# Moving the causal mask of an attention stage from a TensorE product into VectorE's row-minimum instructions

## The reference

```
def attn(x, latent_w, latent_b, Wd_w, Wd_b, out_w, out_b):   # x is layer-normalised
    Wdkv = x @ latent_w + latent_b                            # [b, t, 72], keys and values at once
    q = einsum('btc,hcl->bhtl', x, Wd_w) + Wd_b               # 16 heads
    scores = einsum('bhtl,bsl->bhts', q, Wdkv) / 4            # sqrt(256 / 16)
    scores = where(tril(t, t), scores, -inf)                  # causal
    y = einsum('bhts,bsl->bhtl', softmax(scores), Wdkv)
    return concat_heads(y) @ out_w + out_b
x = x + attn(layernorm(x)); x = x + birwkv(layernorm(x), ctx, ctx, w, u); x = x + experts(layernorm(x))
```

## Time and profile before

| | |
|---|---|
| Runs | 595.64, 602.27, 596.83 us; median 596.83 |
| Span of the profiled execution | 602.4 us (no other time of it is given) |
| PE busy | 524.7 us, 87% |
| DVE busy | 363.1 us, 60% |
| ACT busy | 329.2 us, 55% |
| POOL busy | 314.9 us, 52% |
| 24 to 345 us, the attention: PE, DVE, ACT, POOL busy | 297.19, 221.41, 198.31, 178.85 of 321 us |

### The profile page before, as it was taken

One profiled execution on the slowest core, in us unless ns is written; L12 is line 12 of the kernel. 1 busy time (PEld: TensorE's weight loads), 2 busy tenths in 40 slices (PEclk: granted clock), 3 DMA queues, 4 the chain that ended last, 5 costly groups with the idle time before them and its releaser, 6 DMA issues.

```text
span 602.4 us, 10421 instructions
## 1 busy us (share of the span) xinstructions
PE 524.7 (87%) x3490; PEld 455.9 (76%) x3490; DVE 363.1 (60%) x749; ACT 329.2 (55%) x944; POOL 314.9 (52%) x277
## 2 busy tenths in 40 slices
PE   0898978998999999999899595688997999999691
PEld 0786756876878878888678264588997999999691
DVE  3376696684888776746547634478884787650010
ACT  4376765773677755765554324254784777651120
POOL 3444877535473587622635644064637476644442
PEclk9999999998999999999988879589999999999797
DMA  6405354454365444534302447333958889989610
GB/s 189 166 3 123 58 65 101 57 72 87 57 96 102 65 59 66 105 77 70 64 26 91 111 140 226 124 96 83 280 154 287 210 238 228 235 253 358 176 27 0
DMA packets 53087, 75.65 MB, mean 126 GB/s; under 512 B 10185, under 2 KB 41674, under 8 KB 52778
## 3 DMA queue, kind: packets, MB, share of 16 engines
q1 hardware_dynamic: 43106, 63.91, 41.8%
q0 software_dynamic: 9040, 10.93, 9.6%
q10 hardware_dynamic: 888, 0.15, 0.1%
HBM read 49.29 MB, written 9.49 MB: 98 GB/s over the span
## 4 chain that ended last, share of the span: by engine, by line
PE 39%; DMA 22%; issue 12%; DVE 9%; POOL 9%; ACT 4%; SPq 3%; POOLq 1%; another core or an unknown queue 0%; ACTq 0%
DMA out<-Y,TK 14%; PE P L672 10%; PE PO L796 8%; PE P L750 6%; PE P L768 5%; DMA qT<-qP 3%; POOL out L1717 3%; PE P L758 3%; DMA zP<-ZT 2%; SPq L577 2%; POOL cxa L1690 2%; ACT EB L1011 2%; POOL xs L1676 1%; DMA arena<-wd 1%; PE P L743 1%
## 5 line engine op out<-in xcount | busy, mean ns | idle before, releaser
L1011 ACT ACTIVATE EB<-P,small 128x128 f32<-128x128 f32 x256 | 90.7, 369 | 79.3 <-DVE small L1235 60.1
L1633 POOL TENSOR_TENSOR EB<-EB,small 128x512 f32<-128x512 f32 x64 | 78.9, 1241 | 98.4 <-DVE small L1239 98.2
L672 PE MATMUL P<-GT,WF 128*128 128x256 f32 x768 | 100.8, 290 | 7.2 <-DVE GT L1162 2.6
L672 PEld LDWEIGHTS P<-GT,WF 128*128 128x128 f32 x768 | 96.4, 196 | 8.2 <-DVE GT L1162 3.1
L1717 POOL DMA_INDIRECT out<-Y,TK x39 | 67.4, 1729 | 66.3 <-DMA out<-Y,TK 28.9
L768 PE MATMUL P<-PT,V 128*72 128x512 f32 x128 | 68.7, 619 | 11.2 <-ACT PT L1016 10.1
L750 PEld LDWEIGHTS P<-KT,qT 72*128 72x128 f32 x512 | 67.7, 194 | 12.6 <-DMA qT<-qP 6.8
L750 PE MATMUL P<-KT,qT 72*128 72x128 f32 x512 | 68.9, 278 | 5.4 <-DMA qT<-qP 4.7
L796 PE MATMUL PO<-Ow,zP 128*128 128x256 f32 x270 | 71.2, 407 | 2.0 <-DMA zP<-ZT 1.9
L1250 DVE COPY ZT<-P 72x512 f32<-72x512 f32 x64 | 43.3, 677 | 45.1 <-PE P L768 42.1
L796 PEld LDWEIGHTS PO<-Ow,zP 128*128 128x128 f32 x270 | 52.9, 205 | 17.2 <-issue 10.7
(11 more groups left out here) (237 smaller groups left out, 950.6 us busy)
## 6 DMA issues: line engine op xcount, KB each, us to landing
WR<-wf SPq DMA_DIRECT2D x27, 512.0 KB
arena<-wf SPq DMA_DIRECT2D x24, 512.0 KB
qT<-qP SPq DMA_DIRECT2D x63, 128.0 KB
WS<-wf SPq DMA_DIRECT2D x12, 512.0 KB, 7.4
zP<-ZT SPq DMA_DIRECT2D x80, 72.0 KB
zP<-ZT SPq DMA_DIRECT2D x80, 36.0 KB
X<-x SPq DMA_DIRECT2D x4, 512.0 KB, 6.9
cxa<-ctxin SPq DMA_DIRECT2D x4, 512.0 KB, 5.8
```

Source lines behind the costliest of these rows:

```text
L672: r = e.matmul(o, lt(a), rt_(b), start=start and n == 0, stop=stop and n == 2, skip_group_check=skip)
L1011: e.activation(EB[i][:, j, :], S[:, 128 * j:128 * j + 128], ACT.Exp, bias=NM[i][:, j:j + 1], accum_out=SM[i][:, j:j + 1]).then_inc(s_exp, 1)
L1633: e.tensor_tensor(EB[i][:, :, :], EB[i][:, :, :], SM[i].unsqueeze(2).broadcast_to([128, 4, 128]), ALU.mult).then_inc(s_prob, 1)
```

## The change

The scores are now negated: the query weights and biases are scaled by -0.25 where they were scaled by 0.25. A tile `later` (128 x 128 fp32, 0 on and below the diagonal and 2 to the 100th above it) takes the place of `maskr` and `identr`. PE no longer writes a mask into the bank. DVE adds `later` to each head's negated scores in an instruction that also writes the sum into `EB` (SBUF) and the row minimum into `NM`: four instructions for a unit where one stood. ACT's exponentials read and write `EB` in place, with scale -1 and the minimum as bias, and each waits for its own head's minimum. Since DVE writes `EB`, the wait for the transposes of unit n-3 is DVE's now; and since DVE is the last reader of the bank, PE waits for DVE (`s_max`) where it waited for ACT.

```diff
-        maskr = sb("maskr", [128, 4, 128], f32r, s1)
-        identr = sb("identr", [128, 128], f32r, s1)
+        later = sb("later", [128, 128], fp32, s1)
...
             def scores(n):
...
-                pe.wait_ge(s_cact, ACTC["mask"])
-                pe.wait_ge(s_exp, 4 * (n - 1))
-                e.matmul(S[:, :], identr[:, :], maskr[:, :, :].rearrange("p a b -> p (a b)"), start=True, stop=False, skip_group_check=True)
+                pe.wait_ge(s_max, 4 * (n - 1))
...
                 for j in range(4):
                     p = e.matmul(S[:, 128 * j:128 * j + 128], qT[k % 2][:, 4 * hq + j, c:c + 128], KT[g % 2][:, r:r + 128],
-                                 start=False, stop=True, skip_group_check=True)
+                                 start=True, stop=True)
...
-            ac.wait_ge(s_cpool, POOLC["ident"])
-            e.activation(identr[:, :], ident[:, :], ACT.Copy).then_inc(s_cact, 1)
-            ac.wait_ge(s_cpool, POOLC["mask"])
-            e.activation(maskr[:, :, :], mf, ACT.Copy).then_inc(s_cact, 1)
...
             def exps(n):
-                S, i = SB[n % 2], n % 3
-                ac.wait_ge(s_max, n + 1)
-                ac.wait_ge(s_T, n - 2)
+                i = n % 3
                 for j in range(4):
-                    e.activation(EB[i][:, j, :], S[:, 128 * j:128 * j + 128], ACT.Exp, bias=NM[i][:, j:j + 1], accum_out=SM[i][:, j:j + 1]).then_inc(s_exp, 1)
+                    ac.wait_ge(s_max, 4 * n + j + 1)
+                    e.activation(EB[i][:, j, :], EB[i][:, j, :], ACT.Exp, scale=-1.0, bias=NM[i][:, j:j + 1], accum_out=SM[i][:, j:j + 1]).then_inc(s_exp, 1)
...
             def row_max(n):
+                i = n % 3
+                ve_.wait_ge(s_cpool, POOLC["mask"])
+                ve_.wait_ge(s_T, n - 2)
                 ve_.wait_ge(s_S, n + 1)
-                ve_.wait_ge(s_exp, 4 * (n - 1))
-                e.tensor_reduce(NM[n % 3], SB[n % 2][:, :].rearrange("p (h s) -> p h s", h=4), AX.X, ALU.max, negate=True).then_inc(s_max, 1)
+                for j in range(4):
+                    e.tensor_tensor_reduce(out=EB[i][:, j, :], in0=SB[n % 2][:, 128 * j:128 * j + 128], in1=later[:, :], op0=ALU.add, op1=ALU.min,
+                                           scale=1.0, scalar=3.0e38, accum_out=NM[i][:, j:j + 1]).then_inc(s_max, 1)
...
-            e.affine_select(out=mf, in_=mf, compare_op=ALU.is_ge, fill=-float(2.0 ** 100), base=0,
-                            pattern=[[0, 4], [-1, 128]], channel_multiplier=1).then_inc(s_cpool, 1)
+            e.affine_select(out=later[:, :], in_=later[:, :], compare_op=ALU.is_ge, fill=float(2.0 ** 100), base=0,
+                            pattern=[[-1, 128]], channel_multiplier=1).then_inc(s_cpool, 1)
```

More of the change, by code:

```diff
@@ L402, in build @@
         rLw = arena[:, 2304:2304 + 2 * L].rearrange("p (k l) -> p k l", k=2)
-        mf = EX[:, 0:2, :].rearrange("p a (b s) -> p (a b) s", s=128)
         ut_f = EX[:, 2, 0:128]
@@ L475, in build @@
         IDX = len(POOLC) + NG + 4
-        ACTC = {n: i + 1 for i, n in enumerate(("lw", "identr", "mask", "ut", "onem", "wd", "ew", "eu"))}
+        ACTC = {n: i + 1 for i, n in enumerate(("lw", "ut", "onem", "wd", "ew", "eu"))}
         DVEC = {n: i + 1 for i, n in enumerate(("lw", "wd", "wdb", "wdbh", "ios", "ecap", "jio", "halves", "run"))}
@@ L952, in scalar_program @@
             ac.wait_ge(s_wd, 16)
-            e.activation(Wd[:, 0], rWd, ACT.Copy, scale=0.25).then_inc(s_cact, 1)
+            e.activation(Wd[:, 0], rWd, ACT.Copy, scale=-0.25).then_inc(s_cact, 1)
             def constants():
@@ L1168, in split_weights @@
                 flat = lambda a: a.rearrange("p k m r -> p (k m r)")
-                e.scalar_tensor_tensor(out=flat(Wd[:, 1]), in0=flat(rWd), scalar=0.25, in1=flat(Wd[:, 0].bitcast(fp32)),
+                e.scalar_tensor_tensor(out=flat(Wd[:, 1]), in0=flat(rWd), scalar=-0.25, in1=flat(Wd[:, 0].bitcast(fp32)),
                                        op0=ALU.mult, op1=ALU.subtract).then_inc(s_cdve, 1)
@@ L1173, in constants @@
                 ve_.wait_ge(s_small, N_SMALL)
-                e.tensor_scalar(wdb_s, wdb_s, 0.25, None, ALU.mult).then_inc(s_cdve, 1)
-                e.tensor_scalar(wdbh[0:L, :], wdbh[0:L, :], 0.25, None, ALU.mult).then_inc(s_cdve, 1)
+                e.tensor_scalar(wdb_s, wdb_s, -0.25, None, ALU.mult).then_inc(s_cdve, 1)
+                e.tensor_scalar(wdbh[0:L, :], wdbh[0:L, :], -0.25, None, ALU.mult).then_inc(s_cdve, 1)
                 ve_.wait_ge(s_cpool, POOLC["iota"])
@@ L1592, in gpsimd_program @@
                             pattern=[[-1, 128]], channel_multiplier=1).then_inc(s_cpool, 1)
-            done(e.memset(mf, 0.0))
-            e.affine_select(out=mf, in_=mf, compare_op=ALU.is_ge, fill=-float(2.0 ** 100), base=0,
-                            pattern=[[0, 4], [-1, 128]], channel_multiplier=1).then_inc(s_cpool, 1)
+            done(e.memset(later[:, :], 0.0))
+            e.affine_select(out=later[:, :], in_=later[:, :], compare_op=ALU.is_ge, fill=float(2.0 ** 100), base=0,
+                            pattern=[[-1, 128]], channel_multiplier=1).then_inc(s_cpool, 1)
             e.iota(io.bitcast(i32), pattern=[[0, GB], [1, NE]], base=0, channel_multiplier=0).then_inc(s_cpool, 1)
```

## The result

The changed kernel takes 605.17 us (median of 4 runs, 604.14 to 607.05); the kernel before, beside it, 597.8 us. The ratio is 1.0135, with a 95% interval of 1.0087 to 1.0183. The same file ran again on two chips (which chip the first runs had is not on record), each time beside the kernel before: 1.0267 (1.0199 to 1.0335) and 1.0287 (1.0237 to 1.0337). So the change loses 1.3 to 2.9%, and how much differed from one comparison to the next; the kernel before stands at 598 to 601 us in all. The forecast was 594.0.

A forecast was written before the change was run, and what follows sets the result against it. PE was taken to pace somewhat over half of the attention. Terms -7.7 + 2.6 - 1.4 + 1.0 + 0.7 + 2.0 = -2.8 us, carried over to the 596.83 us median, gave 594.0 us; 8-in-10 range 586 to 605.5.

The forecast's parts named there:

- The moved wait ... +0.7 us: DVE instead of ACT waits for unit n-3's transposes; two such places on the chain, 0.36 us each: +0.7 us.
- What PE loses ... -7.7 us: 64 mask products leave PE; their share on the attention chain, 33 units at 0.235 us, is saved: -7.7 us.
- What DVE gets ... +2.6: Four sums with minimum replace one reduce, +0.52 us a unit; five chain places followed by DVE work: +2.6 us.
- Late next ... +2.0: Fuller DVE makes ZT copies and reciprocals late for PE or SP, 0.5 us in each of four stretches: +2.0 us.
- -1.4: At four chain places ACT's first exponential needs only the first minimum, 0.34 us sooner each: -1.4 us.
- What ACT gets ... +1.0: Exponentials read SBUF instead of PSUM, +0.035 us each, 28 heads on the chain: +1.0 us.
- the second rival: DVE bounds the full attention stretches because each new instruction costs 0.43 us, not 0.28: +8.3 us, 605 us; chance 0.21.
- The third rival: DVE's mask input and POOL contend in SBUF, scalings growing by up to 1.1 us: +8 to +10, 606 us; chance 0.05.
- The first rival: PE's release pays more: earlier exponentials and shorter PE waits for POOL's scaled probabilities, -8.5 us, 588 us; chance 0.29.

The follow-up runs named there:

- the gap closed: Kernel before with unit 24's reciprocal put behind unit 22's ZT copies in DVE's order, so POOL's scaling meets four scans: 1.0011.
- the fillers: Useless transposes before PE's long waits, in the changed kernel with four EB, NM, SM and one DVE wait before scans: 114 gave 0.9948, 146 tuned 0.9880.
- its own fillers: Kernel before, mask product kept, with 77 useless transposes in front of its own long PE waits: 0.9971, clock 0.963.
- fillers at the product's place: Changed kernel with four EB, NM, SM and one DVE wait before scans, plus 96 useless transposes where the mask product stood: 1.0168.
- The pair of kernels with and without DVE's mask: Both with one DVE wait before group 2.1's scans: changed kernel with four EB, NM, SM, 1.0013; kernel before without mask product, 1.0014.
- four buffers: Changed kernel with four EB, NM and SM, so DVE waits for transposes of a unit one further back: 1.0089, again 1.0072.
- The version that reads PSUM: Changed kernel with masked sums written back to PSUM; ACT reads PSUM and waits for all four minima and the transposes itself: 1.0094.
- the scan wait: Changed kernel with four EB, NM, SM; DVE waits before group 2.1's first scan for POOL's pending scaling: 1.0013, again 1.0024.

## Why the prediction was wrong

**"The moved wait ... +0.7 us".** This is the step that failed. Measured, the wait alone costs 2.66% in the kernel before, 15.9 us, and taking it out of the changed kernel gives back 1.8% on one chip and 2.2% on another, 10.6 and 12.9 us. I had counted two places where the wait was on the chain already, each with the time for the sums. What counted was the rest of the same paragraph, "what DVE had queued behind is late by up to 2 us more, but it had a gap of that kind to spare at most places": a wait at the head of an in-order queue held reciprocals, these held POOL, POOL held PE, and behind some of PE's waits its clock fell to half. That path was read at one unit in two traces (152 and 156 us); how the 11 to 16 us divide over the eight to ten waits is not measured. Nor is the collision with the scans at that unit shown to be the price: in the kernel before with the gap closed it cost nothing that could be told.

**"What PE loses ... -7.7 us".** The term did not arrive: without the product, and with nothing else changed, the kernel is at 1.0102. The sum took PE's rate as given. With the product gone PE waits longer and is granted less: 0.940 to 0.945 in place of 0.953 to 0.955 in all unfilled kernels where only the product is missing or replaced. That the lower clock takes a part of the gain back is what the fillers speak for: with them the kernels without the product are at 0.9948 and 0.9880. That it takes all of it is not shown. The kernel before, whose clock rose by 0.010 with its own fillers, gained next to nothing (0.9971), and filled against filled the product's removal is worth 0.2% in one pair and 1.8% in the other, where 7.7 us would be 1.3%. Nor is it shown why the clock is lower without the product: fillers at the product's place left it at 0.942. I had read the clock column only in the four stretches of the earlier trace rows, where it is 1.00. In before's own row for a later stretch it was there to be seen:

```profile
264.00:324.00 60.00, 57.24 (x339) 46.85 (x338) 33.83 (x106) 33.56 (x126) 24.56 (x24) 0.91 0.33 68
```

**"What DVE gets ... +2.6" and "Late next ... +2.0".** Too large. A unit costs DVE 0.25 us more, not 0.52, so five places make 1.3 us; its busy time from 24 to 345 us went from 221.4 to 233.3 us, 12 us and not 33. The pair of kernels with and without DVE's mask (1.0013 and 1.0014) shows no cost that could be told.

**"-1.4", the earlier exponentials.** Right in direction; it shows with four buffers (ACT's wait 40.1 us) and is hidden in the changed kernel by the moved wait (52.8).

**"What ACT gets ... +1.0".** About right. The exponential lasts 387 ns where it lasted 367, but what the engine pays is the distance from one start to the next, and this went from 0.34 us to 0.385:

```profile
65.00 0.39 ACT L1002 ACTIVATE EB<-EB,small 128x128 f32<-128x128 f32 x1
...
65.38 0.39 ACT L1002 ACTIVATE EB<-EB,small 128x128 f32<-128x128 f32 x1
```

Over all neighbours in the two traces the medians are 343 and 385 ns, 42 ns where I took 35, so 28 heads make +1.2 us. The Trainium skill, VectorE: DVE Perf Modes, section "The TRN2 errata — SBUF-src ops pay a fixed extra latency per instruction", gives cycle counts from which the estimate was 43 ns: the trace agrees. The version that reads PSUM has 343 ns again, and its time is no shorter (1.0094 against 1.0089); it differs in more than the source.

**The rivals.** The time, 605.2, is the number of the second rival (DVE as the bound), and this is an accident: the new instruction is at 0.21 us and not at its 0.43, and DVE is not full. The third rival, DVE's mask input against POOL, did not happen either: the median scaling is 1042 ns before and after. The scalings that grew did so beside scans, on a larger scale. That agrees with the Trainium skill, SBUF — State Buffer, section "Who interferes with whom": a VectorE instruction with two SBUF inputs contends with a GpSimd instruction that reads SBUF, and one with at most one, outside the two-port modes, does not. The first rival had the mechanism for a gain that the kernel with fillers at last shows, and missed what takes it back. No rival priced the moved wait, and none the clock.

**What stays open.** Whether the scan wait is worth 0.5%. Why the clock is lower without the product, and how much of the -7.7 us the clock takes. Why the changed kernel loses 1.35% in its first comparison and 2.7 to 2.9% in two others, where its clock is lower too (0.943 against 0.932 and 0.935). And the experts: from their first product to the end the changed kernel takes 238.4 us without and 231.6 us with fillers in the two traces shown, though the fillers all stand ahead of them, and the clock column over this stretch is 0.91 in both; this part of the gain is seen and not explained. From the last exponential to the end the traces of this case take from 256.6 to 267.3 us, so single executions differ here by as much as the effects that were looked for.

## What to carry to other kernels

When a wait moves to another engine, list what stands behind it in that engine's queue and who waits for each of these, and price the longest of these paths, not the place where the wait itself is on the chain. Before counting work that is taken from TensorE as a gain, read the granted clock over the whole stage: here the kernels with less work waited longer and had a lower clock, and useless products in the waits were worth trying (131 of them made the changed kernel 2.9% faster; in the kernel before 77 of them gave nothing that could be told). Take sizes from repeated runs beside each other; a trace of one execution that lies 0.9% over its median hides an effect of that size.

## What the hardware showed that I had not expected

- TensorE's granted clock fell to 0.50, 1.2 of 2.4 GHz, in these traces mostly behind waits of 0.9 to 6.2 us, and not behind each of them; which wait brings a fall differed between kernels. It also fell without one: in the changed kernel PE had no wait from 317.1 to 323 us, did 16 products of 8 columns from 319.7 on and then transposes and scores, and the clock fell at about 322.7; the kernel before fell likewise at about 320.6. The Trainium skill, TensorE: Matmul & The Clock Gate, section "Part 1: The HAM clock gate (the "warmup" mystery)", has the two levels, and the row at 158 us agrees.
- Time and clock go together from run to run of one and the same kernel: of 35 runs of the kernel before on one chip the fastest is 591.58 us at a clock of 0.967, and the two above 603 us are at 0.947 and 0.940.
- A GpSimd scaling that starts 0.42 us ahead of four VectorE scans takes 5.86 us and ends 0.85 us after the last of them: of its 1.04 us of work it gets next to nothing done during 4.6 us of scans.
- A sum with minimum on VectorE, 128 columns from PSUM and SBUF, takes 282 ns and its read 81, and starts every 0.21 us; written back to PSUM it is 318 and 138 ns, and starts every 0.25 us.
